# Seven score products from period 8 on, and more homes for the last units of P, in a graph attention kernel on one core

## The reference

```
lQ = m @ Wlq;  lK = h @ Wlk;  lV = h @ Wlv + blv
gQ = m @ Wgq;  gK = mean(h) @ Wgk;  gV = mean(h) @ Wgv + bgv
es = m @ Wes;  eV = m @ Wev + bev
local = where(adj, lQ @ lK.T * s, -1e9)          # 4096 x 4096
top   = max(rowmax(local), gQ @ gK.T * s, es)
le, ge, ee = exp(local - top), exp(gQ @ gK.T * s - top), exp(es - top)
den   = sum(le) + ge + ee
res   = le/den @ lV + ge/den * gV + ee/den * eV
out   = x + max(res, m)
```

## Time and profile before

| | |
|---|---|
| median of 3 runs | 731.57 us (731.06 to 731.91) |
| the profiled execution | 731.89 us, its span 730.0 us |
| TensorE (PE) busy | 722.1 us, 99% |
| VectorE (DVE) busy | 564.5 us, 77% |
| ScalarE (ACT) busy | 532.3 us, 73% |
| GpSimd (POOL) busy | 433.6 us, 59% |
| chain that ended last | PE 81%, issue 5%, DVE 5%, POOL 4%, ACT 3%, DMA 2% |

### The profile page before, as it was taken

The page is one execution under the profiler, slowest core; times in us unless marked ns, Lnnn a source line. Parts: engine busy times, 40 slices in busy tenths (PEclk is TensorE's granted clock), DMA queues, the critical chain, the costliest instruction groups (busy, mean ns, idle before and its releaser), DMA issues.

```text
span 730.0 us, 15027 instructions
## 1 busy us (share of the span) xinstructions
PE 722.1 (99%) x5248; PEld 511.8 (70%) x5248; DVE 564.5 (77%) x1347; ACT 532.3 (73%) x709; POOL 433.6 (59%) x300
## 2 busy tenths in 40 slices
PE   8999999999999999999999999999999999999998
PEld 7667566667766777776767677776776767676777
DVE  6975988777887788878878787878878887977643
ACT  6885967858677776776788677777777677677690
POOL 4779889455465455555555564556545555654493
PEclk9999999999999999999999999999999999999999
DMA  9782877869779888968878798989888798878697
GB/s 299 135 178 76 162 154 148 160 139 214 158 159 176 168 162 152 202 146 189 154 175 165 159 190 142 203 150 180 175 171 159 158 198 146 184 160 188 115 170 166
DMA packets 364716, 121.93 MB, mean 167 GB/s; under 512 B 324832, under 2 KB 364640, under 8 KB 364640
## 3 DMA queue, kind: packets, MB, share of 16 engines
q1 hardware_dynamic: 364096, 120.44, 81.7%
q10 hardware_dynamic: 544, 0.52, 0.2%
HBM read 36.57 MB, written 4.19 MB: 56 GB/s over the span
## 4 chain that ended last, share of the span: by engine, by line
PE 81%; issue 5%; DVE 5%; POOL 4%; ACT 3%; DMA 2%; DVEq 0%; SPq 0%; ACTq 0%; POOLq 0%
PE ps_u L1124 13%; PE ps_u L1128 13%; PE ps_u L1126 13%; PE ps_x L1022 6%; PE ps_x L1023 6%; PE ps_x L1021 6%; PE ps_q L945 4%; PE ps_v L1021 3%; PE ps_v L1023 3%; PE ps_v L1022 3%; POOL p_base L619 2%; PE ps_w L1021 2%; PE ps_w L1022 2%; PE ps_w L1023 2%; DVE st L1339 1%
## 5 line engine op out<-in xcount | busy, mean ns | idle before, releaser
L619 POOL TENSOR_TENSOR p_base<-s,p_base 128x1024 f16<-128x1024 f32 x112 | 242.4, 2164 | 229.4 <-ACT p_base L822 220.4
L1124 PE MATMUL ps_u<-v_rows,pT_base 128*128 128x256 f16 x968 | 263.8, 273 | 0.7 <-DMA pT_base<-bias 0.7
L1128 PE MATMUL ps_u<-v_rows,pT_base 128*128 128x256 f16 x968 | 263.8, 273 | 0.0
L1126 PE MATMUL ps_u<-v_rows,pT_base 128*128 128x256 f16 x968 | 263.8, 273 | 0.0
L785 ACT ACTIVATE bias<-adj,big 128x1024 f32<-128x1024 uint8 x127 | 156.5, 1237 | 130.5 <-DVE bmax L1492 128.5
L798 ACT ACTIVATE s<-s,negm,invc 128x1024 f32<-128x1024 f32 x128 | 157.0, 1227 | 8.9 <-DVE negm L1548 8.9
L822 ACT ACTIVATE p_base<-s 128x1024 f16<-128x1024 f32 x122 | 129.0, 1057 | 6.2 <-DMA hW<-p_base 1.3
L1124 PEld LDWEIGHTS ps_u<-v_rows,pT_base 128*128 128x128 f16 x968 | 94.7, 98 | 53.2 <-DMA pT_base<-bias 0.9
L1126 PEld LDWEIGHTS ps_u<-v_rows,pT_base 128*128 128x128 f16 x968 | 94.7, 98 | 52.2
L1492 DVE CUSTOM_DVE_ANT_0 s<-ps_x,bias 128x512 f32<-128x512 f32 x128 | 87.1, 685 | 48.1 <-PE ps_x L1023 44.6
L1128 PEld LDWEIGHTS ps_u<-v_rows,pT_base 128*128 128x128 f16 x968 | 94.7, 98 | 11.0
(11 more groups left out here) (242 smaller groups left out, 1262.4 us busy)
## 6 DMA issues: line engine op xcount, KB each, us to landing
adj<-adj SPq DMA_DIRECT2D x64, 256.0 KB, 3.2
pT_base<-p_base SPq DMA_TRANSPOSE x238, 3.2
s<-x SPq DMA_DIRECT2D x7, 512.0 KB, 7.8
f32q<-mx SPq DMA_DIRECT2D x14, 256.0 KB, 3.7
xm<-x SPq DMA_DIRECT2D x14, 256.0 KB, 3.1
xm<-mx SPq DMA_DIRECT2D x14, 256.0 KB, 3.5
out<-t_sb SPq DMA_DIRECT2D x14, 256.0 KB, 2.5
mxT_f<-mxT SPq DMA_DIRECT2D x4, 256.0 KB, 3.2
```

The lines of the kernel that those rows point to most:

```text
L619: nc.gpsimd.tensor_tensor(p_rows(u)[:, 1], s32[:, p % NS, u % 2], p_rows(u)[:, 0], ALU.subtract).then_inc(s_plo, 1)
L1124: nc.tensor.matmul(acc, turn[:, 0, j], v_rows[:, kc, 0:D], start=opens, stop=False, skip_group_check=True)
L1126: nc.tensor.matmul(acc, turn[:, 0, j], v_rows[:, kc, D:2 * D], start=False, stop=False, skip_group_check=True)
L1128: done = nc.tensor.matmul(acc, turn[:, 1, j], v_rows[:, kc, 0:D], start=False, stop=end, skip_group_check=True)
```

## The change

- PC goes from 12 to 8: pairs 2 to 15 have seven products, and pair 2 has its own `q_sums` and seven forms of Q.
- VectorE makes P's low halves only for units 0 to 3 (`LOWS`), where it made them for units 0 to 9; GpSimd makes the rest.
- On GpSimd, the key forms of group 1 are all in period 4, those of group 2 in periods 6, 7 and 8, those of group 3 in periods 9, 10 and 11, each behind the low halves of its period.
- T3 of groups 0 and 1 is made in period 6, of group 2 in period 8, of group 3 in period 10 (before: 10, 10, 12, 12), on TensorE, ScalarE and VectorE alike.
- In a period with seven products p7 stands behind three slots of P times V (before: two), p5 behind seven, directly ahead of p6 (before: four).
- From unit MORE = LAST - 3 = 117 on, P is transposed in one instruction for both halves, behind the low half; units 117 to 122 go to six homes in hW, 123 to 125 to pT, 126 and 127 to the first two in hW again: nine homes. Units 117 to 121 wait for the p4 that last reads the part of hW in question.
- The two loads for the last rows are issued together in period 64 (before: one in 63, one in 64).
- On VectorE, `mx_scale` comes first in a classic period of its kind, and the subtractions of blv from period 7 come at that period's end.

```diff
@@ -30,7 +30,8 @@
     NPER = NP * NG
-    PC = 12
+    PC = 8
+    LOWS = 4
     QH = 3
@@ -40,6 +41,8 @@
     END = LAST - 4
+    MORE = LAST - 3
+    MORE_HOMES = 9
     SCALE = float(D) ** -0.5
@@ -191,7 +194,7 @@
         s_pT = [sem(f"s_pT{i}") for i in range(NPT)]
-        s_pT_end = [sem(f"s_pT_end{i}") for i in range(2 * NG)]
+        s_pT_end = [sem(f"s_pT_end{i}") for i in range(MORE_HOMES)]
         s_pT_low = [sem(f"s_pT_low{i}") for i in range(NPT)]
@@ -253,7 +256,7 @@
         def low_on_dve(u):
-            return u // 2 + LAG_E < PC - 2
+            return u < LOWS
 
@@ -304,9 +307,9 @@
         def p_turned(u):
-            if u < LAST or u >= LAST + 6:
+            if u < MORE or MORE + 6 <= u < MORE + MORE_HOMES:
                 return pT[:, u % NPT]
-            return pT_more[:, u - LAST]
+            return pT_more[:, (u - MORE) % MORE_HOMES]
 
@@ -320,7 +323,7 @@
         def turned(u):
-            return (s_pT[u % NPT], ring(u, NPT)) if u < LAST else (s_pT_end[u - LAST], 16)
+            return (s_pT[u % NPT], ring(u, NPT)) if u < MORE else (s_pT_end[(u - MORE) % MORE_HOMES], ring(u - MORE, MORE_HOMES))
 
@@ -365,16 +368,16 @@
 
-                sp.wait_ge(*((s_plo, u + 1) if u >= LAST else (s_phi, u + 1)))
-                if u >= LAST + 6:
-                    sp.wait_ge(s_pv, LAST - 1)
-                elif u >= LAST:
-                    sp.wait_ge(s_p4, NPER)
+                sp.wait_ge(*((s_plo, u + 1) if u >= MORE else (s_phi, u + 1)))
+                if u >= MORE + 6:
+                    sp.wait_ge(s_pv, u - MORE_HOMES + 1)
+                elif u >= MORE:
+                    sp.wait_ge(s_p4, NPER - 2 + max(u - MORE - 2, 0) if u < MORE + 5 else NPER)
                 elif u >= NPT:
...
                     sp.wait_ge(s_gstep, 1)
-                if u >= LAST:
+                if u >= MORE:
                     sp.dma_start_transpose(p_turned(u).rearrange("p a c q -> p (a c) q"),
@@ -500,10 +503,10 @@
                     load_rows(NP - 2)
-                if p in (NPER - 1, NPER):
-                    i = p - NPER + 1
-                    sp.wait_ge(s_bias, 2 * (NPER - 1 + i))
-                    sp.dma_start(edge_rows[:, i], (x_pairs, mx_pairs)[i][NP - 1]).then_inc(s_xm_end, 16)
+                if p == NPER:
+                    for i, src in enumerate((x_pairs, mx_pairs)):
+                        sp.wait_ge(s_bias, 2 * (NPER - 1 + i))
+                        sp.dma_start(edge_rows[:, i], src[NP - 1]).then_inc(s_xm_end, 16)
             store(NP - 3)
@@ -612,7 +615,7 @@
                     pool.wait_ge(s_plo, u)
-                if END + 5 <= u < LAST + 5:
+                if END + 5 <= u < MORE + 5:
                     pool.wait_ge(*turned_low(u - 5))
@@ -661,11 +664,16 @@
                     finish(n)
-                if p in (4, 6, 8):
-                    keys_t1(p // 2 - 1)
-                    keys_t2(p // 2 - 1)
-                if p in (5, 7, 9):
-                    keys_t4((p - 3) // 2)
+                if p == 4:
+                    keys_t1(1)
+                    keys_t2(1)
+                    keys_t4(1)
+                if p in (6, 9):
+                    keys_t1(p // 3)
+                if p in (7, 10):
+                    keys_t2(p // 3)
+                if p in (8, 11):
+                    keys_t4((p + 1) // 3 - 1)
             pool.wait_ge(s_xm_end, 32)
@@ -823,6 +831,8 @@
                 act.wait_ge(s_t3sum, g + 1)
+                act.wait_ge(s_t1, g + 1)
+                act.wait_ge(s_p7, PC - NG + g + 1)
                 nc.scalar.activation(plain(g, 0, 1, 0), ps_q[:, g % 2].rearrange("p (j q) -> p j q", q=P), ACT.Copy
@@ -924,9 +934,11 @@
                     p_high(u + 1)
-                if p in (PC - 2, PC):
-                    keys_t3_high(p - PC + 2)
-                    keys_t3_high(p - PC + 3)
+                if p == PC - 2:
+                    keys_t3_high(0)
+                    keys_t3_high(1)
+                if p in (PC, PC + 2):
+                    keys_t3_high(p // 2 - 2)
                 if p % NG == 3 and QH <= (p + 5) // NG < NP:
@@ -966,7 +978,7 @@
                 if n == PC // NG + 1:
-                    pe.wait_ge(s_t3, NG)
+                    pe.wait_ge(s_t3, 3)
                 if n >= QH:
@@ -1103,7 +1115,7 @@
                         pe.wait_ge(*turned(u))
-                        if u < LAST:
+                        if u < MORE:
                             pe.wait_ge(*turned_low(u))
@@ -1133,9 +1145,10 @@
                 if g < 2:
-                    pe.wait_ge(s_qf, PC - 3)
+                    pe.wait_ge(s_qf, 7)
                 else:
-                    pe.wait_ge(s_c2, 2)
+                    pe.wait_ge(s_qf, 2 * g + 3)
+                    pe.wait_ge(s_t3, g)
                 for k, (c, hl) in enumerate(((1, 0), (1, 1), (0, 0), (0, 1))):
@@ -1143,7 +1156,7 @@
                 if n == 0:
-                    pe.wait_ge(s_t3, 2)
+                    pe.wait_ge(s_t3, NG)
                 if n < QH:
@@ -1287,28 +1300,26 @@
                         p1(p)
-                    p_times_v(p, 0, 2)
+                    p_times_v(p, 0, 3)
                     if wino(old):
                         p7(old)
-                    p_times_v(p, 2, 4)
-                    if p < NPER:
-                        p5(p)
-                    p_times_v(p, 4, 6)
-                    if p == PC:
-                        keys_t3_sum(2)
-                        keys_t3_sum(3)
+                    p_times_v(p, 3, 6)
+                    if p in (PC, PC + 2):
+                        keys_t3_sum(p // 2 - 2)
                     if p == NPER:
...
                     if p < NPER:
+                        p5(p)
                         p6(p)
-                    p_times_v(p, 7, 9)
-                    if es:
-                        es_values((p - 11) // NG)
+                    p_times_v(p, 7, 8)
                     if p == NPER + 1:
...
                         es_values_end()
+                    p_times_v(p, 8, 9)
+                    if es:
+                        es_values((p - 11) // NG)
                     if wino(old) and p < NPER:
@@ -1743,10 +1754,6 @@
                     side_top(1)
-                if p == 7:
-                    dve.wait_ge(s_gev, 5)
-                    nc.vector.tensor_tensor(gv_b[:, :], gv_b[:, :], blv_b[:, :], ALU.subtract).then_inc(s_gev, 1)
-                    nc.vector.tensor_tensor(bev_b[:, :], bev_b[:, :], blv_b[:, :], ALU.subtract).then_inc(s_gev, 1)
                 u = 2 * (p - LAG_E)
@@ -1758,12 +1765,12 @@
                         p_low(u)
+                    if step == 3:
+                        mx_scale((p + 5) // NG)
                     out11(p)
...
                         p_low(0)
-                    if step == 3:
-                        mx_scale((p + 5) // NG)
                     if project:
@@ -1775,27 +1782,18 @@
                         q_row_scales(m)
-                    if p == 8:
-                        row_max(1)
                     if p == 5:
...
                         weights_low()
-                    if p == 9:
-                        wev_low()
-                    if step == 1 and p >= 9:
-                        weights((p - 9) // NG)
-                    if step == 2 and p >= 10:
-                        side_rows((p - 10) // NG, 0)
-                        side_rows((p - 10) // NG, 1)
-                    if step == 3 and p >= 11:
-                        es_rows((p - 11) // NG)
-                        local_rows((p - 11) // NG)
+                        dve.wait_ge(s_gev, 5)
+                        nc.vector.tensor_tensor(gv_b[:, :], gv_b[:, :], blv_b[:, :], ALU.subtract).then_inc(s_gev, 1)
+                        nc.vector.tensor_tensor(bev_b[:, :], bev_b[:, :], blv_b[:, :], ALU.subtract).then_inc(s_gev, 1)
                 else:
                     done = (p - 9) // NG
-                    ended = done < NP - 1
+                    ended = 0 <= done < NP - 1
                     if wino(old):
@@ -1814,9 +1812,8 @@
                         add12(p)
-                    if p == PC:
-                        keys_t3_low(2)
-                        keys_t3_low(3)
+                    if p in (PC, PC + 2):
+                        keys_t3_low(p // 2 - 2)
                     if wino(old):
@@ -1834,6 +1831,8 @@
                         row_max(n)
+                    if p == 9:
+                        wev_low()
                     if step == 1 and ended:
```

## The result

The changed kernel takes 735.04 us (median of four runs, 734.92 to 735.24), the kernel before 731.65 in the same rounds (731.06 to 731.91). The ratio is 1.0048 with a 95% interval of 1.0036 to 1.0061: slower by 3.4 us. The forecast was 727.6, in a range from 725.4 to 731.0. The profiled executions have spans of 733.5 and 730.0 us, a difference of 3.5.

The account below looks back on a forecast made before the run. TensorE, busy 99% of the span, was taken as the bound. 731.89 - 2.59 - 1.09 - 2.07 + 1.8 = 727.9, less 0.32: 727.6 us, in a range from 725.4 to 731.0.

Parts of the forecast that it names:

- (d): Steady periods: the later fifth product closes the 1.09 us hole of period 19 and costs nothing, bound 2.4.
- (b): Start: GpSimd's longer queue makes key form T2(3) late, so the sixth product of period 11 waits 1.8 us.
- (c): Start of period 8: unit 5's low half, now on GpSimd, comes in time; 0 us lost, bounds 0 and 1.0.
- (a): Periods 8 to 11: seven products for eight take 2.59 us off TensorE; VectorE's added adds cost nothing.
- (e): Tail: nine homes and whole-unit transposes close three holes of 0.86, 0.51 and 0.70 us, 2.07 in all.
- Rival 2: Tail: the holes stay, as waits for ScalarE and GpSimd; 729.7 us, chance 0.12.
- rivals, 1: Start: GpSimd is in time with its key forms; 725.8 us, chance 0.20.
- Rival 3: Start: GpSimd is late by 4.5 to 7 us; 730.3 to 732.8 us, no change, chance 0.12.
- Rival 4: Start: moved low halves lock VectorE out, delaying row maximum and exponentials; slower, 734.3 us if T2(3) ends at 142, chance 0.08.
- I am wrong if VectorE ends a wait of TensorE in every fourth period: Changed trace: a sign, named beforehand, that would show the forecast wrong; no size given.

Follow-up runs that it names:

- s_swap: Changed kernel; in periods 9 and 10 ScalarE's first exponential and high half precede the mask, GpSimd's T1(3) between period 9's low halves: 733.36 us.
- e_t1_first: p5_early with GpSimd making T1(3) ahead of the two low halves of P of period 9: 732.67 us.
- e_lows6: p5_early with six low halves of P on VectorE instead of four: 731.37 us.
- e_t3_late: p5_early with VectorE's low half of T3, periods 8 and 10, behind out11 and not before out21: 732.80 us.
- p5_early: Changed kernel with the fifth and seventh products back in their earlier places: 732.13 us.
- s_all3: s_all2 with six low halves of P on VectorE instead of four: 729.11 us.
- p5_late_alone: Kernel before the change with only the fifth and seventh products moved later: 737.10 us.
- s_side1: Changed kernel with the first side row moved to the end of a pair's second period, from the second pair on: 730.91 us.
- e_both: p5_early with the edits of both e_t1_first and e_t3_late: 732.85 us.
- s_all2: s_side1 and s_swap together, Wev weight halves in period 13 in place of 9, GpSimd's T4(3) right behind T2(3): 730.05 us.

## Why the prediction was wrong, step by step

The terms of the sum come to -3.95 us, and the spans differ by +3.46: 7.4 us apart. Of these, 3.4 belong to the start (5.18 measured, 1.8 expected) and 4.0 to the steady periods (0 expected). Step (d) is what turned the sign; (b) and (c) used up 5.2 of the 5.75 us that (a), (d) and (e) were to bring.

(a) The columns: 2.59 us, right; the difference of the spans closes with it. "Cost nothing" for VectorE's added adds: in no hole of the changed kernel does TensorE wait for one of them. What its other small instructions cost, once GpSimd makes the low halves, is in (c).

(b) Mis-sized. The mechanism, GpSimd's late T2(3), was right. The prediction wanted it at 133.5 and had it at 135.3; it came at 137.9, 4.4 late, and the holes up to p6(11) make 0.75 + 2.42 + 1.31 = 4.48. s_swap gives the same sum: T2(3) 1.6 late, holes of 1.58. GpSimd's 57.6 us from 80.3 on, against the 55.0 worked out: five forms 26.3 (25.8 expected), Q's low halves 4.4 (3.8), Q's sums 4.0 (3.6), low halves of P 17.2 (17.1), masked x 1.2 (1.2), and waits for ScalarE 5.0 (3.5); the durations overlap by some 0.5 us in all. The largest term that failed is the estimate of 1.5 for units 8 and 9, which was 3.9; the 0.9 for unit 5 did not come. I had named the mask that waits for VectorE and not followed it to the block (4.28 us of ScalarE's idle time at 110.06). e_t1_first shows that another order of GpSimd's queue wins nothing while that stands, and e_lows6 that two low halves less in the queue leave that wait and the holes of period 11. The forms' own working had a slip of 0.1: two T1 of 5.50 and three of 4.54 are 24.6, not 24.5. Behind p6(11), T4(3) and Q's transpose cost 0.29 and 0.41 more, which no step had. The hole before p1(11) came by a road that no step had: VectorE takes out21(9) behind T3's low half, which waits for ScalarE, which waits for GpSimd's Q's sums. e_t3_late shows that it is the same loss seen earlier.

(c) 0 expected within 0 to 1.0; 0.75 lost. It gave GpSimd no time in return: in e_lows6, without it, the holes of period 11 are as in p5_early. e_lows6 and s_all3 put it to the two low halves of units 4 and 5 on GpSimd, and the changed kernel's trace shows how. These run from 92.21 to 96.42; 96.4 was expected. VectorE has `mx_scale` at the head of period 7 now, and two of its smallest instructions are held, one by each of the two low halves:

```profile
92.31 2.05 DVE L1481 TENSOR_SCALAR mscale<-mcl 128x2 int32<-128x2 int32 x1
...
94.47 1.98 DVE L1488 TENSOR_TENSOR mu<-mpow,unw 128x4 f32<-128x4 f32 x1
96.37 0.68 DVE L1503 CUSTOM_DVE_ANT_0 s<-ps_w,bias 128x512 f32<-128x512 f32 x1
```

In e_lows6 the same two take 0.17 and 0.16 us. So four blocks followed the low half of unit 5 and not two, out22(7) ended at 98.9 and not at 97.8, and that is the hole. It is the mistake of (d) once more, in another place.

(d) The step that turned the sign. Its gain in period 19 is there in the changed kernel (1.09), but p5_late_alone shows that the move of the product does not close that hole by itself. Its cost was put at nothing, with a bound of 2.4, from "add12 and out21 can move by up to 0.98" against 1.04 of room. Measured: 2.9 us between p5_early and the changed kernel, 4.03 of holes there, 5.4 in p5_late_alone. What failed is taking 0.98 for an upper bound of the delay: behind the delayed add stood two instructions that GpSimd can hold for 2 us each, and one of the two had begun just ahead of GpSimd before. The Trainium skill, "SBUF — State Buffer", section "Who interferes with whom", says that a VectorE instruction with two SBUF inputs and a GpSimd instruction that reads SBUF lock each other out for a whole instruction. I applied that to the key forms, not to the side rows. By it, a shift of 0.98 turns 0.48 + 2.24 into two held ones, and the trace agrees: 1.89 and 1.99. s_side1, which keeps the late product and moves the row, takes back all 4.0.

(e) 2.07, right, in the changed kernel and alone. Rival 2 is out.

Of the rivals, 1 falls with T2(3) at 137.9. Rival 3 wanted GpSimd late by 4.5 to 7 us; it was 4.4 late, and the start's 5.18 by itself gives 731.57 - 5.75 + 5.18 = 731.0, inside its band of no change; p5_early, with the 1.09 of period 19 back, measured 732.1. So rival 3 was near the truth on the start, and its total fails only by (d). Rival 4 named VectorE held by GpSimd, but with its decision at 139.3 and by way of the row maximum; the slower result came by another instruction and in other periods. "I am wrong if VectorE ends a wait of TensorE in every fourth period" is what happened, in every eighth.

What stays open: why GpSimd's low half comes alternately 4.52 and 5.17 us into the period from period 34 on, so that both halves of the side row are held in every second pair only; what part of the last 2.9 us of s_all3 is VectorE's small operations; and what the swap on ScalarE is worth without T1(3)'s new place.

## What to carry to other kernels

When an edit delays an instruction, add up what may lengthen behind it, not only the delay: list the instructions up to the one that is waited for, mark those that another engine can hold, and ask which of them used to slip through just before that engine began. Room of 1 us against a shift of 1 us is no room when one of them can cost 1.5 more. And a wait seen on a queue's engine is worth following through the in-order neighbours (mask before exponential before low half) before the queue is shortened: three edits around the queue (e_t3_late, e_t1_first, e_both) moved holes about, and the edit with the swap on the engine upstream moved T2(3) and the time.

## What the runs showed of the hardware

- A VectorE instruction that takes 0.48 us alone took 1.89, 1.99, 2.23 and 2.24 beside GpSimd operations of 2.07 to 2.31 us on SBUF. Two GpSimd operations in a row hold two in a row, one each.
- The size of the VectorE operation is no protection: one on 128x2 values and one on 128x4 took 2.05 and 1.98 us beside two low halves in the changed kernel, and 0.17 and 0.16 without them in e_lows6; two on 128x2 took 1.20 and 2.04 in s_all2. The blocks and adds with one operand in PSUM ran in 0.67 to 0.69 in the same stretches.
